# Attention scores from fp32r value-and-remainder pairs instead of float32 products, in a fused attention and mixture-of-experts kernel

## The reference, cut to what matters

```python
scores = jnp.einsum('bkgsd,bktd->bkgst', qh, kh) / scale     # qh: heads of layernorm(x), kh: heads of ctx
weights = jax.nn.softmax(scores, axis=-1)
out = jnp.einsum('bkgst,bktd->bkgsd', weights, vh)
x = x + tanh(g_xattn) * out                                  # then a second layernorm gives z
logits = tanh(z @ Wg1.T) @ Wg2.T                             # two of 8 experts for each row
x = x + tanh(g_ffn) * sum_of_two(top_scores * (silu(z @ Wup.T + bup) @ Wdown.T + bdown))
```

## Time and profile before

| | |
|---|---|
| median of 3 runs | 698.03 us (696.45 to 698.19) |
| profiled execution, its own time | 695.72 us |
| its span, first to last instruction | 693.9 us |
| PE / PEld busy over the span | 91% / 62% |
| DVE / ACT / POOL busy over the span | 75% / 55% / 51% |
| granted TensorE clock, mean | 0.978 |

### The profile page before, as it was taken

How to read it: one execution, slowest core, us unless ns; L and a number is a source line. 1 busy time by engine, 2 the same in 40 slices (tenths; PEclk the granted TensorE clock), 3 DMA queues, 4 the chain that set the end, 5 groups by cost and what they waited for, 6 DMA issues and landing times.

```text
span 693.9 us, 17038 instructions
## 1 busy us (share of the span) xinstructions
PE 634.2 (91%) x5064; PEld 432.1 (62%) x5064; DVE 521.6 (75%) x1456; ACT 378.3 (55%) x692; POOL 353.8 (51%) x538
## 2 busy tenths in 40 slices
PE   3779999999999999999999977899999999999970
PEld 2435555555555555555555466789998888888850
DVE  3468888888888888888888455476767788887763
ACT  2267777777767676767676531333334544544430
POOL 4123545464545455656665536890032666575454
PEclk9999999999999999999999989899999999999995
DMA  3123344444444444444432677344665999999977
GB/s 103 53 66 116 114 141 149 139 142 141 144 140 144 140 144 141 145 141 145 143 126 77 208 279 256 109 154 152 215 227 177 304 348 345 348 354 352 334 250 256
DMA packets 65032, 129.40 MB, mean 186 GB/s; under 512 B 8640, under 2 KB 12736, under 8 KB 64704
## 3 DMA queue, kind: packets, MB, share of 16 engines
q1 hardware_dynamic: 44496, 77.35, 32.9%
q0 software_dynamic: 10368, 33.56, 14.3%
q10 hardware_dynamic: 10096, 17.59, 7.8%
HBM read 74.20 MB, written 54.26 MB: 185 GB/s over the span
## 4 chain that ended last, share of the span: by engine, by line
PE 77%; DVE 11%; issue 4%; DMA 2%; POOL 2%; ACT 1%; SPq 1%; DVEq 0%; ACTq 0%; POOLq 0%
PE s_ps L1281 13%; PE bank_a L1260 8%; PE st_ps L1304 8%; DVE nmax L993 7%; PE st_ps L1398 5%; PE st_ps L1399 5%; PE st_ps L1400 5%; PE s_ps L1379 4%; PE bank_c L1221 3%; PE bank_b L1269 3%; PE st_ps L1312 3%; PE bank_q L1356 2%; PE bank_a L1411 2%; PE bank_a L1412 2%; PE bank_a L1410 2%
## 5 line engine op out<-in xcount | busy, mean ns | idle before, releaser
L993 DVE TENSOR_REDUCE nmax<-s_ps 128x8 f32<-128x1024 f32 x128 | 156.4, 1222 | 62.3 <-PE s_ps L1281 61.2
L754 ACT ACTIVATE probs<-st_ps 128x1024 f32<-128x1024 f32 x128 | 131.2, 1025 | 67.2 <-PE st_ps L1312 63.6
L1281 PE MATMUL s_ps<-k_t,q_t 32*128 32x256 f32 x1024 | 151.9, 415 | 17.2 <-DVE nmax L993 14.4
L1304 PE MATMUL st_ps<-q_t,k_t 32*128 32x512 f32 x512 | 145.6, 645 | 0.3
L1281 PEld LDWEIGHTS s_ps<-k_t,q_t 32*128 32x128 f32 x1024 | 92.6, 192 | 68.9 <-DVE nmax L993 44.7
L695 POOL DMA_INDIRECT y<-expert_out,rows_all x64 | 64.6, 1009 | 57.7 <-DMA expert_out<-y_sb 43.3
L1398 PE MATMUL st_ps<-w_hi,zh 128*128 x284 | 86.9, 306 | 1.3 <-DVE zl L1092 1.3
L1399 PE MATMUL st_ps<-w_lo,zh 128*128 x284 | 80.7, 284 | 0.0
L1400 PE MATMUL st_ps<-w_hi,zl 128*128 x284 | 80.5, 283 | 0.0
L831 ACT ACTIVATE t_sb<-u_sb 128x256 f32<-128x256 f32 x71 | 29.7, 418 | 87.1 <-DVE u_sb L1102 78.1
L656 POOL DMA_INDIRECT slots<-z,slot_i x64 | 64.6, 1009 | 16.0 <-issue 15.7
(11 more groups left out here) (182 smaller groups left out, 1376.6 us busy)
## 6 DMA issues: line engine op xcount, KB each, us to landing
expert_out<-y_sb SPq DMA_DIRECT2D x71, 256.0 KB, 3.9
z_s<-slots ACTq DMA_DIRECT2D x67, 256.0 KB, 3.9
x_in<-in_x SPq DMA_DIRECT2D x32, 256.0 KB, 2.7
wst<-in_w SPq DMA_DIRECT2D x32, 256.0 KB, 2.6
x_res<-in_x SPq DMA_DIRECT2D x32, 256.0 KB, 2.8
x_scratch<-x_res SPq DMA_DIRECT2D x32, 256.0 KB, 2.0
r_in<-x_scratch SPq DMA_DIRECT2D x32, 256.0 KB, 5.4
out<-r_in SPq DMA_DIRECT2D x32, 256.0 KB, 5.1
```

Source lines behind the costliest of these rows:

```text
L754: a.activation(out, st_ps[:, :].rearrange("t (k n) -> t k n", k=2), ACT.Exp, scale=HD ** -0.5).then_inc(exp_done[half], 1)
L993: v.tensor_reduce(out, s_ps[:, :].rearrange("s (r g c t) -> s r g c t", r=2, g=2, c=2), X_AXIS, ALU.max, negate=True).then_inc(max_done, 1)
L1281: last = t_.matmul(s_ps[:, HALF * rr + 2 * P * gg:HALF * rr + 2 * P * (gg + 1)], q_t[r2][row:row + ROWS32, P * g_:P * (g_ + 1)], k_t[r2][r ...
L1304: t_.matmul(st_ps[:, HALF * rr:HALF * (rr + 1)], k_t[r][row:row + ROWS32, P * i:P * (i + 1)], q_t[r][row:row + ROWS32, :], start=True, sto ...
```

## The change

- Scores and transposed scores are computed with fp32r products. A query becomes a fp32r value and the fp32r remainder, and the 16 + 16 numbers of one head fill the 32 rows of a row group. The keys stand there twice as values, or twice as remainders. Query pair times key values plus query pair times key remainders, added in PSUM, is one score: two products with 32 rows in place of a float32 one. A head now needs its own 128 columns, so `s_ps` is filled by eight products of 128 moving columns in each of two row groups (`score(n)`), and `st_ps` by two products of 512 columns in each of two (`across(part)`), and the bf16 products are as before.
- ACT rounds keys (`k_hl`, 256 columns) and queries (`q_hl`, 512 columns) to fp32r, POOL computes the remainders (`k_lo_done`, `q_lo_done`), and PE turns all of them with fp32r products against a fp32r identity: four for the keys, twice four for the queries (`query_rows(0)`, `query_rows(1)`), in place of one and four float32 transposes. ACT copies 512 columns of keys and twice 512 of queries out of PSUM, where it copied twice 128 and 512.
- The second weighted sum moves between the two `query_rows`, and the order of the exponentials' halves in `probs` changes. The normalised queries share a buffer with `z_t`. `q_t`, `k_t`, `v_aug` have 3 buffers instead of 4, `y1`, `y2` of phase 2 have 4 instead of 3, and the DMA scratch is 8192.
- All steps are written out; there is no hardware loop.

```diff
-YRING = 3
+YRING = 4
+TRING = 3
-def pipeline(eng, step, steps, first, last, unroll):
-    for s in range(first):
-        step(s, s % unroll)
-    with eng.Fori(0, (last - first) // unroll) as i:
-        for u in range(unroll):
-            step(i * unroll + (first + u), (first + u) % unroll)
-    for s in range(last, steps):
+def pipeline(step, steps, unroll):
+    for s in range(steps):
         step(s, s % unroll)
...
+        def keys_twice(t):
+            return t[:, :].rearrange("p (k d) -> p k d", d=HD).unsqueeze(2).to_broadcast([P, KV, 2, HD])
+        def q_half(i):
+            return q_hl[:, :].rearrange("p (n i d) -> p n i d", i=2, d=HD)[:, :, i, :]
...
         def _(pool):
                 if valid(b1):
+                    pool.wait_ge(k_hi_done, b1 + 1)
+                    g.tensor_tensor(k_hl[:, 2 * P:4 * P].rearrange("p (k u d) -> p k u d", u=2, d=HD),
+                                    keys_twice(c_in[u1]),
+                                    k_hl[:, 0:2 * P].bitcast(F32).rearrange("p (k u d) -> p k u d", u=2, d=HD),
+                                    ALU.subtract).then_inc(k_lo_done, 1)
                     pool.wait_ge(w_hi_done, b1 + 1)
...
+                if valid(b1):
+                    pool.wait_ge(q_hi_done, b1 + 1)
+                    g.tensor_tensor(q_half(1), q_n[:, :].rearrange("p (n d) -> p n d", d=HD),
+                                    q_half(0).bitcast(F32), ALU.subtract).then_inc(q_lo_done, 1)
...
         def _(act):
+                def keys(b):
+                    act.wait_ge(kt_done, b + 1)
+                    wait(act, st_done[1], 2 * (b - TRING) + 2)
+                    a.activation(k_t[r1][:, :], bank_c[:, :], ACT.Copy).then_inc(kt_copied, 1)
+                def queries(b, c):
+                    act.wait_ge(qt_done, 2 * b + c + 1)
+                    a.activation(q_t[r1][:, c * D:(c + 1) * D], (bank_q, bank_c)[c][:, :],
+                                 ACT.Copy).then_inc(qt_copied, 1)
+                if valid(b1):
+                    act.wait_ge(c_loaded[p1_], ring2(b1, p1_))
+                    wait(act, kt_done, b1)
+                    a.activation(k_hl[:, 0:2 * P].rearrange("p (k u d) -> p k u d", u=2, d=HD),
+                                 keys_twice(c_in[p1_]), ACT.Copy).then_inc(k_hi_done, 1)
...
                 if valid(b4):
                     exps(b4, 1, 1)
+                if valid(b1):
+                    act.wait_ge(n_done, b1 + 1)
+                    wait(act, qt_done, 2 * b1)
+                    a.activation(q_half(0), q_n[:, :].rearrange("p (n d) -> p n d", d=HD), ACT.Copy).then_inc(q_hi_done, 1)
+                if valid(b4):
                     o_out(b4, 0)
+                if valid(b3):
+                    exps(b3, 0, 0)
                 if valid(b1):
+                    keys(b1)
+                    queries(b1, 0)
+                if valid(b4):
+                    o_out(b4, 1)
+                if valid(b1):
+                    queries(b1, 1)
...
         def _(pe):
+                def query_rows(c):
+                    for g_ in range(G):
+                        last = t_.matmul((bank_q, bank_c)[c][:, P * g_:P * g_ + P], heads_of(q_hl, g_, c),
+                                         ident_r[:, :], start=True, stop=True)
+                    last.then_inc(qt_done, 1)
...
-                    def part(gg):
+                    def score(n):
+                        gg, c, part_ = n // 4, n // 2 % 2, n % 2
+                        g_ = 2 * i + gg
                         for rr in range(2):
-                            row, g_ = ROWS32 * (2 * half + rr), 2 * i + gg
-                            last = t_.matmul(s_ps[:, HALF * rr + 2 * P * gg:HALF * rr + 2 * P * (gg + 1)],
-                                             q_t[r2][row:row + ROWS32, P * g_:P * (g_ + 1)],
-                                             k_t[r2][row:row + ROWS32, :], start=True, stop=True,
-                                             tile_position=(row, 0))
+                            row, at = ROWS32 * (2 * half + rr), HALF * rr + P * (2 * gg + c)
+                            last = t_.matmul(s_ps[:, at:at + P],
+                                             q_t[r2][row:row + ROWS32, c * D + P * g_:c * D + P * (g_ + 1)],
+                                             k_t[r2][row:row + ROWS32, (2 * part_ + c) * P:(2 * part_ + c + 1) * P],
+                                             start=(part_ == 0), stop=(part_ == 1), tile_position=(row, 0))
                         return last
+                    def across(part_):
+                        for rr in range(2):
+                            row = ROWS32 * (2 * over + rr)
+                            t_.matmul(st_ps[:, HALF * rr:HALF * (rr + 1)],
+                                      k_t[r][row:row + ROWS32, (2 * part_ + i) * P:(2 * part_ + i + 1) * P],
+                                      q_t[r][row:row + ROWS32, i * D:(i + 1) * D], start=(part_ == 0), stop=False,
+                                      tile_position=(row, 0))
...
-    nc = bacc.Bacc("TRN2", target_bir_lowering=False, num_devices=1)
+    nc = bacc.Bacc("TRN2", target_bir_lowering=False, num_devices=1, dynamic_dma_scratch_size=8192)
```

More of the change, by code:

```diff
@@ L425, in _ @@
             g.memset(tick[:, :], 1.0).then_inc(const_ready, 1)
-            for i in range(RING):
+            for i in range(TRING):
                 g.memset(v_aug[i][:, :], 0.0).then_inc(const_ready, 1)
@@ L780, in step @@
                 if valid(b3):
[L781 to L785, removed]
-                        a.activation(k_t[r1][:, i * P:(i + 1) * P], bank_c[:, 0:P], ACT.Copy,
-                                     scale=parity[:, i:i + 1]).then_inc(kt_copied, 1)
-                    act.wait_ge(qt_done, b1 + 1)
-                    a.activation(q_t[r1][:, :], bank_q[:, :], ACT.Copy).then_inc(qt_copied, 1)
-                if valid(b4):
-                    o_out(b4, 1)
-                if valid(b3):
                     exps(b3, 0, 1)
                 if valid(b5):
+                    act.wait_ge(q_lo_done, b1 + 1 if valid(b1) else B)
                     gate_rows(b5)
@@ L1301, in scores @@
                             pe.wait_ge(nmt_copied, b + 1)
-                        for rr in range(2):
-                            row = ROWS32 * (2 * over + rr)
-                            t_.matmul(st_ps[:, HALF * rr:HALF * (rr + 1)],
-                                      k_t[r][row:row + ROWS32, P * i:P * (i + 1)],
-                                      q_t[r][row:row + ROWS32, :], start=True, stop=False, tile_position=(row, 0))
-                    if valid(b2):
-                        part(1).then_inc(s_done, 1)
+                        across(0)
+                    if valid(b2):
+                        for n in range(1, 4):
+                            score(n)
+                    if valid(b):
+                        across(1)
+                    if valid(b2):
+                        for n in range(4, 7):
+                            score(n)
                     if valid(b):
@@ L1341, in step @@
                     rows_back(b4, 0)
-                    weighted_sum(b4, r4, 1)
                 if valid(b1):
-                    pe.wait_ge(c_loaded[p1_], ring2(b1, p1_))
+                    pe.wait_ge(k_lo_done, b1 + 1)
                     if valid(b6):
                         pe.wait_ge(lg_copied, b6 + 1)
-                    elif valid(b5 - 1 if ends else 0):
+                    elif valid(b5 - 1):
                         pe.wait_ge(zt_copied, b5)
-                    t_.transpose(bank_c[:, 0:P], c_in[p1_][:, :], ident_f[:, :]).then_inc(kt_done, 1)
-                    pe.wait_ge(n_done, b1 + 1)
+                    elif valid(b2):
+                        pe.wait_ge(qt_copied, 2 * b2 + 2)
+                    for n in range(4):
+                        last = t_.matmul(bank_c[:, P * n:P * n + P], heads_of(k_hl, n // 2, n % 2), ident_r[:, :],
+                                         start=True, stop=True)
+                    last.then_inc(kt_done, 1)
                     if valid(b3):
@@ L1353, in step @@
                     elif valid(b2):
[L1354 to L1357 removed]
+                        pe.wait_ge(qt_copied, 2 * b2 + 1)
+                    pe.wait_ge(q_lo_done, b1 + 1)
+                    query_rows(0)
+                if valid(b4):
+                    weighted_sum(b4, r4, 1)
+                if valid(b1):
+                    pe.wait_ge(kt_copied, b1 + 1)
+                    query_rows(1)
                 scores(3)
```

105 lines of the change are left out of this document (55 added, 50 removed).

## The result

The changed kernel takes 736.86 us (median of 4 runs, 730.96 to 742.66) where the kernel before takes 697.24 in the same session: 1.0549 times as long, with a 95% interval from 1.0498 to 1.060. One run, 742.66, was in a slower state and is left out of the ratio. The profiled execution is the longest of the other three: 739.84 us, span 738.1.

The account below looks back on a forecast made before the run. A phase 1 step was taken as 7.52 us of PE and 4.00 of DVE. 27 steps at +0.77 (20.8), filling 1.6, start 3.0, draining -3.0 and loop -1.8 gave +20.6: 719 us beside the median, range 690 to 768.

Parts of the forecast that it names:

- the forecast's own case: Whole kernel: 719 us beside the median, own range 705 to 733, chance 0.63.
- What sets a product's price: 0.11 for the load: PE's short fp32r products: a 128-column load takes 0.11 us against 0.05 for the stream, so the load decides.
- the third rival: PE's fp32r products: load and product do not overlap, 0.16 a product, +2.0 us a step, about 752; chance 0.05.
- cheaper loads: PE's fp32r loads 0.05 to 0.06 apart: a call takes 0.80, about 682 us in all; chance 0.13.
- short streams at the float32 rate: PE's short fp32r products: 128 columns at 0.21, a call 1.92, 16.4 us a step, about 840; chance 0.07.
- 1.04 a call: One call of `scores`: eight loads in the `s_ps` groups make it 1.04 us, where it took 1.29 before.
- Where the 0.25 of two calls goes: Ahead of `rows_back`: the 0.50 us saved is lost waiting for `o_sb`, behind the rounding of the queries.
- Keys and queries, and the step of +0.77: PE from `rows_back` to the last maximum: 12 fp32r products replace 5 transposes; with the rest, +0.77 us a step.
- The queries' remainder hides, just: POOL's remainder of the queries ends at 89.85, 0.15 us before PE asks for it at 90.0.
- the second rival: POOL's remainder is late: at twice 1.25 us PE waits 1.1 a step, about 749 in all; chance 0.12.
- The start, +3.0: Ahead of the first scores: rounding 0.6, remainder 1.27, four more products and a second copy, 3.0 us in all.
- The first steps, 0 with bounds of -7 and +3: First two steps, calls of 2.10 us: no net change; -7 if loads stay at 0.11, +3 if they double.

Follow-up runs that it names:

- the two halves: Changed kernel with 64 of 128 query columns loaded per `s_ps` product: 724.42 us, ratio 1.0365; with 64 of 128 key columns streamed instead: 747.46 us, ratio 1.0695.
- the kernel with three buffers: Changed kernel with three instead of four y buffers in phase 2, the smaller descriptor memory kept: 734.98 us, ratio 1.0535 to the kernel before.
- the keys' remainder later: Changed kernel with POOL's remainder of the keys moved behind the residual's add, from ahead of the weights' remainder: 737.72 us, ratio 1.0529 to the kernel before.
- both edits: Changed kernel with ACT's copy `o_sb` first, PE reordered, and POOL's keys' remainder behind the residual's add: 723.64 us, ratio 1.0389 to the kernel before.
- fewer loads: Kernel with both edits, plus the maximum from rounded keys alone (4 loads, not 8) and unused bf16 products in PE's early waits: 706.56 us, ratio 1.0128.

## Why the prediction was right, and where it was too small

The direction, the mechanism and the range held: slower, because twelve products of keys and queries cost more than the calls give back, with 736.86 against 719 and an upper end of 768; but that is above the 705 to 733 that the forecast's own case had. The sum was +20.6 and the span grew by 44.2. By the steps of the prediction:

- *What sets a product's price: 0.11 for the load.* Right, and shown by the two halves. In the same rows pairs of loads follow each other 0.11 apart in one row group while its products stream. The Trainium skill ("TensorE: Matmul & The Clock Gate", Part 3) says that a weight load overlaps with matmuls in flight only when the row group differs; these rows do not bear it out, and the third rival (0.16 a product) falls. The rivals of cheaper loads (0.05) and of short streams at the float32 rate (0.21) fall with it.
- *1.04 a call.* Right (222.82 to the next instruction at 223.86).
- *Where the 0.25 of two calls goes: the wait for `o_sb`.* The wait is the right one, as the copy put first shows, but `rows_back` starts 0.29 later than worked out (4.32 instead of 4.03 after `scores(1)`). 0.18 of it is the rounding's start, which I took as 2.88 after `scores(1)` and which is 3.06. I had moved POOL's add by 0.7 and not asked what lies beside it then. It is the normalising, for which the rounding waits: that takes 0.11 more, and starts 0.02 later after `scores(1)` than before, where I had it 0.07 earlier. The other 0.11 are the two copies (0.54 apart, not 0.49) and 0.14 from the copy's end to PE, not 0.06.
- *Keys and queries, and the step of +0.77.* From `rows_back` to the maximum 4.26 were worked out, 4.17 measured; DVE's stretch of 4.00 stayed. 0.77 + 0.29 - 0.09 = 0.97, and the steps are 0.98 longer than 11.52.
- *The queries' remainder hides, just.* True of 17 steps, with no slack. In the ten with tables it does not, and the second rival holds there with 0.27 a step: I read POOL's work from a step without tables.
- *The start, +3.0.* Measured +4.4. I left out that `w_lo` stands ahead of the queries' remainder on POOL (9.17 to 10.46): the remainder starts at 10.41 and could have started at about 9.2, behind that of the keys.
- *The first steps, 0 with bounds of -7 and +3.* The mis-sized term: +11.7. Loads do double (16 products in 1.97), so the first two steps cost +3.1, the upper bound; but the lower level also lasted to 68.6 instead of 35.0, so that steps three and four cost 8.6 where 1.6 stood. How long it lasts differs (49 to 85 us in the kernels with all eight loads of 128 columns), and not by the program alone: the kernel with three buffers has the same instructions in phase 1, its level rose at 52 in the execution profiled, and its four steps cost +6.5. So some 5 of the 11.7 us belong to this execution.
- *The draining steps, -3.0*: measured -3.0, in part by luck. On the chain the `st_ps` products of a call went from 1.06 to 1.13 down to 0.66 to 0.74, not to 0.54, so six calls give 2.4; where the rest comes from is not shown. *The loop, -1.8*: measured -1.9. *The fourth buffer, 0*: nothing against it, within a spread of 5 us that phase 2 has by itself.

What stays open is what raises the level and what lets it fall. Transposes in the waits had it high from 11.3 to 14.7 us and then not until 48.8, dense streams to 21.5 in one kernel and to 13.2 in another, and no run here separates these. A kernel's level is known from one profiled execution each.

## What to carry to other kernels

Count weight loads, not streamed columns, when products get short: here halving a product's stream was worth 0.02 us a step, since each brought a load of the same 0.11. When an instruction is added to POOL, everything behind it on POOL moves, and the question is what DVE is doing at the new time. And a wait that is seen in a trace is a cost only if nothing else is as late: taking away a collision of 0.7 us on DVE gave nothing, while putting ACT's copy `o_sb` ahead of the rounding, with PE's order to match, gave 0.37 a step.

## What the runs showed of the hardware that I had not expected

- DVE's normalising ends a fixed time after the POOL instruction beside it. It takes 0.54 us by itself. In the steady steps of four kernels it ends 0.28 to 0.29 after that POOL instruction (218.51 after 218.22 in the changed kernel), and takes 0.65, 0.74, 0.73 and 1.09 there: in the changed kernel, with the keys' remainder later, with both edits, and with fewer loads. The small `m` with its two SBUF inputs ends 0.03 to 0.04 after POOL's `w_lo`, in the kernel before too (85.35 after 85.32); it takes 0.10 in steps where `w_lo` does not lie beside it, 0.27 in that step, and 0.96 in the changed kernel. The Trainium skill ("SBUF — State Buffer", Who interferes with whom) says that a DVE instruction with two SBUF inputs contends with a POOL instruction that reads SBUF, by an exclusive lock; the trace agrees for `m`.
- At the lower level the rows' granted clock can read 1.00 (10 to 68 us of the changed kernel), while loads are 0.2 apart and not 0.11.
- Where unused products had brought the upper level first, it fell again with PE working, by the granted clock: at 14.7 us with the transposes, at 21.5 and 13.2 with the dense products.
